# A four-layer graph network on one core: the last LayerNorm, gamma, beta and residual move into the edge pass

## The reference, cut to what matters

```python
h = relu(layernorm(x))
feat = concat([h[src], edge_attr])                 # 100000 x 131
m    = gelu(feat @ W1 + b1) @ W2 + b2              # one message per edge
t    = h + segment_sum(m, dst)                     # 6250 x 128
x    = x + layernorm(t) * gamma + beta             # the output
```

## Time and profile before

| | us |
|---|---|
| median of 3 runs | 6101.89 (6098.71 to 6105.08) |
| the profiled execution | 6096.41 |
| its span, first to last instruction | 6094.7 |
| first step of the edge pass on DVE | 5111.58 |
| last window of the edge pass on DVE | 6053.81 |
| first gather of the edge pass | 5071.93 |
| last gather of the edge pass begins | 6037.01 |

### The profile page before, as it was taken

One profiled execution on the slowest core, in us unless ns is written; L12 is line 12 of the kernel. 1 busy time (PEld: TensorE's weight loads), 2 busy tenths in 40 slices (PEclk: granted clock), 3 DMA queues, 4 the chain that ended last, 5 costly groups with the idle time before them and its releaser, 6 DMA issues. The chain is left out here.

```text
span 6094.7 us, 132845 instructions
## 1 busy us (share of the span) xinstructions
PE 3875.0 (64%) x27584; PEld 3373.1 (55%) x27585; DVE 3724.8 (61%) x9159; ACT 1637.2 (27%) x4058; POOL 4523.9 (74%) x5174
## 2 busy tenths in 40 slices
PE   1555555555555476776789989946666664666765
PEld 1444545445554365655578878845555553545543
DVE  6333333566666677777887787775555555555555
ACT  1000000122121333333455565531111113222222
POOL 6777777677777677777778888857777775777775
PEclk9667666666666688888899999977777776888887
DMA  4222222222222355555577777732222221222222
GB/s 123 69 69 72 71 69 72 62 71 69 72 69 71 104 178 170 174 174 169 174 241 251 248 225 248 251 105 69 71 72 69 71 70 54 72 72 74 70 72 96
DMA packets 457819, 701.26 MB, mean 115 GB/s; under 512 B 94129, under 2 KB 214334, under 8 KB 456690
## 3 DMA queue, kind: packets, MB, share of 16 engines
q0 software_dynamic: 126336, 260.69, 16.6%
q10 hardware_dynamic: 210816, 255.92, 12.9%
q1 hardware_dynamic: 120434, 182.52, 9.2%
HBM read 506.59 MB, written 189.53 MB: 114 GB/s over the span
## 5 line engine op out<-in xcount | busy, mean ns | idle before, releaser
L865 POOL DMA_INDIRECT u_parts<-table,src x3096 | 2921.3, 944 | 1057.8 <-issue 942.9
L941 PE MATMUL ps_sum<-u_parts,onehot 128*128 x2928 | 651.8, 393 | 687.7 <-SPq L720 575.3
L1480 DVE SCALAR_TENSOR_TENSOR onehot<-dst,minus_row,beside 128x512 f32<-128x512 f32 x1100 | 817.4, 744 | 362.2 <-issue 290.0
L941 PEld LDWEIGHTS ps_sum<-u_parts,onehot 128*128 128x128 f32 x2928 | 574.5, 292 | 763.5 <-issue 762.7
L865 POOL DMA_INDIRECT ring<-table,src x774 | 737.6, 953 | 265.4 <-issue 232.0
L941 PEld LDWEIGHTS ps_sum<-msg,onehot 128*128 128x128 f32 x4896 | 689.6, 212 | 302.3 <-issue 152.8
L941 PE MATMUL ps_u<-u_parts,onehot 128*128 x2928 | 537.6, 345 | 464.3 <-SPq L720 414.7
L941 PE MATMUL ps_sum<-msg,onehot 128*128 128x128 f32 x4896 | 748.3, 301 | 124.6 <-DVE msg L528 93.6
L941 PEld LDWEIGHTS ps_u<-u_parts,onehot 128*128 128x128 f32 x2928 | 477.7, 248 | 511.4 <-issue 510.6
L1779 DVE TENSOR_TENSOR zu<-ps_u,ring 128x512 f32<-128x512 f32 x732 | 502.6, 687 | 339.5 <-SPq L720 161.2
L1019 PE MATMUL ps_u<-WE_attr,attr_t 128*128 128x512 f32 x488 | 317.6, 739 | 324.5 <-ACT attr_t L1337 324.5
(11 more groups left out here) (207 smaller groups left out, 6446.1 us busy)
## 6 DMA issues: line engine op xcount, KB each, us to landing
ring<-z_rows SPq DMA_DIRECT2D x392, 256.0 KB, 3.5
ring<-table SPq DMA_DIRECT2D x4096, 0.5 KB
hot_rows<-hots ACTq DMA_DIRECT2D x244, 256.0 KB
hots<-hot_rows ACTq DMA_DIRECT2D x244, 256.0 KB, 3.4
z_rows<-ring SPq DMA_DIRECT2D x196, 256.0 KB
u_parts<-table,src POOLq DMA_INDIRECT x3096
table<-hots ACTq DMA_DIRECT2D x122, 256.0 KB
wide<-hot_rows ACTq DMA_DIRECT2D x122, 256.0 KB, 3.3
```

What stands on the lines that cost most here:

```text
L865: nc.gpsimd.indirect_dma_start(out=slot(p, c % slots)[:, t * P:(t + 1) * P], out_offset=None, in_=tables[p], in_offset=bass.IndirectOffset ...
L941: last = nc.tensor.matmul(sums[k % len(sums)][:, 0:P], lhsT=(onehot[:, k % HOTS, :, :] if hots_of is None else hots_of)[:, t, :], rhs=rows ...
L1480: V.scalar_tensor_tensor(out=buffers[k % len(buffers)], in0=per_row(dst[:, ds(chunk * TILES, TILES)], [P, TILES, P]), scalar=minus_row0[:, ...
```

## The change

The tail behind the edge pass goes away; its work runs per window inside the pass, with the same helpers as in the mean pass.

```diff
@@ act: edge pass
                 if on(k, 7) and have(7):
                     copy_turned(s, 3, 7)
                 if on(k, 11) and have(11):
-                    store_window(s, y_rows[:, blocks_at(act, s, 11, chunk), :], win_y, win_out,
-                                 s.back(11) + (3 * STEPS + UNROLL))
-            over_steps(act, ENGINE.Activation, body, 11)
-            norm_rows(x, acc, groups=0)
-            for g in SCALAR_NORMS:
-                act.wait_ge(y_in[g // 4], 16)
-                norm_group(x, acc, ACT.Identity, g)
+                    root_window(s, 2, 11)
+                if on(k, 13) and have(13):
+                    act.wait_ge(win_rows_ready, s.back(13) + 2 * STEPS)
+                    norm_window(s, 2, 13, win_y, blocks_at(act, s, 13, chunk), ACT.Identity)
+                if on(k, 15) and have(15):
+                    store_window(s, out.rearrange("p (b f) -> p b f", f=P)[:, blocks_at(act, s, 15, chunk), :],
+                                 win_rows, win_rows_ready, s.back(15) + (2 * STEPS + UNROLL))
+            over_steps(act, ENGINE.Activation, body, 15)
@@ dve: edge pass
                 if on(k, 10) and have(10):
                     win = blocks_at(dve, s, 10, chunk)
-                    dve.wait_ge(rows_stored, s.back(10).in_rounds(16, 16 * WINDOWS * 3))
+                    dve.wait_ge(win_normed, s.back(10) + 2 * STEPS)
                     V.tensor_tensor(win_y, x[:, win, :], product_of(s, 3, 10), ALU.add)\
                      .then_inc(win_out, UNROLL)
...
-            over_steps(dve, ENGINE.DVE, edge_body, 10)
+                    window_moments(s, 3, 2, 10, win_y)
+                if on(k, 12) and have(12):
+                    window_scales(s, 2, 12, blocks_at(dve, s, 12, chunk))
+                if on(k, 14) and have(14):
+                    at = s.back(14)
+                    win = blocks_at(dve, s, 14, chunk)
+                    dve.wait_ge(win_normed, at + (2 * STEPS + UNROLL))
+                    V.tensor_tensor(scaled_p, win_h, ga_p.unsqueeze(1).to_broadcast([P, GROUP, P]), ALU.mult)\
+                     .then_inc(win_biased, UNROLL)
+                    dve.wait_ge(win_biased, at + (3 * STEPS + UNROLL))
+                    dve.wait_ge(rows_stored, at.in_rounds(16, 16 * WINDOWS * 3))
+                    V.tensor_tensor(win_rows, scaled_p, h[:, win, :], ALU.add).then_inc(win_rows_ready, UNROLL)
+            over_steps(dve, ENGINE.DVE, edge_body, 14)
```

More of the change, by code:

```diff
@@ L235, in build @@
         caps_p = ps_c[:, 0:GROUP * CAPS]
-        ga_p = beside[:, 0:P]
+        ga_p = beside[:, P:2 * P]
+        scaled_p = ps_c[:, :].rearrange("p (t f) -> p t f", f=P)
         plain_sums = (ps_sum[0], ps_sum[1], ps_u[0], ps_u[1])
@@ L251, in build @@
         hot_rows = nc.dram_tensor("hot_rows", [STEPS, P, 2 * TILES * P], bf16, kind="Internal").ap()
-        y_rows = nc.dram_tensor("y_rows", [P, NB * P], fp32, kind="Internal").ap()\
-            .rearrange("p (b f) -> p b f", f=P)
         z_rows = nc.dram_tensor("z_rows", [CHUNKS, P, TILES * P], fp32, kind="Internal").ap()
@@ L332, in build @@
         h_in = [sem(f"h_in{q}") for q in range(PIECES)]
[L333 to L336, removed]
         root_in = sem("root_in")
@@ L585, in build @@
         CUTS = [(g, min(g + 4, GROUPS)) for g in range(0, GROUPS, 4)]
-        assert len(CUTS) == len(y_in)
-        VECTOR_NORMS = (3, 7, 11, 12)
-        SCALAR_NORMS = [g for g in range(GROUPS) if g not in VECTOR_NORMS]
         NORMED = [0, GROUPS, GROUPS + NORM_GROUPS, 2 * GROUPS + NORM_GROUPS]
@@ L766, in _ @@
             sp.wait_ge(rows_stored, 16 * WINDOWS * 4)
[L767 to L774, removed]
         @block.gpsimd
@@ L870, in _ @@
                     messages(2, messages(1))
[L872 to L875, removed]
         @block.tensor
@@ L1870, in _ @@
             V.tensor_copy(bo_p, BO[:, :])
+            V.tensor_copy(ga_p, GA[:, :])
             link(V.tensor_copy(bt_p, BT[:, :]))
@@ L1911, in edge_body @@
-                    last.then_inc(win_counted, UNROLL)
-                    dve.wait_ge(win_counted, s.back(10) + (STEPS * 2 + UNROLL))
-            over_steps(dve, ENGINE.DVE, edge_body, 10)
-            dve.wait_ge(step_added, STEPS * (EDGE + 1))
[L1915 to L1930, removed]
+                    window_moments(s, 3, 2, 10, win_y)
```

## The result

| | before | after |
|---|---|---|
| median | 6102.89 us (6098.71 to 6105.08, 6 runs) | 6204.43 us (6201.39 to 6211.07, 6 runs) |
| span of the profiled execution | 6094.7 us | 6201.2 us |
| mean granted clock | 0.790 | 0.787 |

The changed kernel takes 1.0168 times as long (95% interval 1.0157 to 1.0179), 101.5 us more. The forecast was 6272 us, +170. The direction, the bound and the range held; the size of the step per round did not.

A forecast was written before the change was run, and what follows sets the result against it. POOL's gathers at 15.8 us a round bound the kernel, with the steps' ring of waits at 15.34 close behind; 3.6 us a round added 192.2, the end took 22.2, the gamma copy added 0.3: 6272 us, range 6200 to 6420.

The forecast's parts named there:

- The bound and the ring: Edge pass: waits passing between DVE, ACT and PE set each round's 15.34 us; work on them lengthens it one for one.
- POOL's slack: Edge pass: the steps' rounds take 15.34 us against 15.8 for POOL's gathers, so half a microsecond a round is free.
- Term 1: DVE behind `bn_stats`: six small operations from statistics to variance delay the next one-hot and `zu`, 1.0 us a round.
- Term 2: DVE behind the variance: two 128x512 operations for gamma and residual, 1.7 us a round, bounds 1.3 and 2.1.
- Term 3: DVE at age 12: two small scale operations fall where it waits 2.57 us for PE, costing nothing.
- Term 4: ACT between Gelu and `attr_t`: four norm activations of 1.65 us, nearly covered, 0.2 us a round, bounds 0 and 0.6.
- Term 5: ACT behind the copy: square root and two table loads, mostly covered by other waits, 0.2 us a round, bounds 0 and 1.6.
- Term 6: ACT's loop head: loading 20 table values instead of 16 and new windows' addresses, 0.5 us a round, bounds 0.1 and 0.9.
- Sum: Edge pass: all additions per round together, 3.6 us, lengthening a round from 15.34 to 18.94 us.
- Rival D: Edge pass: fewer of the additions count, 2.3 us a round, giving 6197 us; chance 0.03.
- rival B: PE in the edge pass: longer idling delays TensorE's return to 2.4 GHz, 1.9 us more a round, 6382 us; chance 0.06.
- The end: From the fifty-ninth window's statistics to the span's end: 30.4 us instead of 52.6, as the tail and POOL's last additions go.

The follow-up runs named there:

- e2: Changed kernel with one more 128x512 DVE operation between the gamma product and the residual, where the next one-hot and `zu` are waited for: 6233.5 us, 1.0208 times before.
- e3: Changed kernel with one more 128x512 DVE operation in the step before `zu`, where DVE waits for PE anyway: 6209.49 us, 1.0167 times before.
- e7: Kernel before with only the six small variance operations added behind `bn_stats` in every window, results unused: 6180.66 us, 1.0135 times before.
- e1: Changed kernel with Copy in place of the window's square root, so 122 table loads go: 6205.99 us, 1.016 times before.
- e8: Kernel before with the 13 last additions on DVE instead of POOL: 6091.3 us, 0.9989 times before.
- e4: Changed kernel with gamma and residual moved to age 17, a step with idle time, and the store to age 19: 6167.12 us, 1.0097 times before.

## Why the prediction was right, and where it was off

- *The bound and the ring.* Right. POOL's slack of half a microsecond was all there was; e2 and e3 show that place counts. The rounds did not lie 18.5 to 19.5 us apart but 17.1 to 18.9. POOL waited 87 us for slots and not 190, and its last gather begins at 6112.6, not near 6230. That has two causes. The mis-sized step is 67 us of it. The rest is POOL's lead, which the prediction left as it was: before, the last gather begins 5 us ahead of the fifty-ninth window's statistics (6037.0 and 6042.11), now 57 us ahead (6112.6 and 6169.46), since a bound of slots lets POOL keep its ring full.
- *Term 1, six small operations, 1.0.* Right: 1.10, and 1.20 where they stand alone (e7).
- *Term 2, gamma and residual, 1.7.* Too high: 1.36 (2.46 - 1.10), close to the lower bound of 1.3. The first of the pair follows the small ones without a gap, and only the second waits, for 0.24. Two gains had no term at all, 0.16 ahead of `win_y` and 0.13 up to the end of `bn_stats`. Together with them this term carries 0.6 of the error.
- *Term 3, scales.* Right, nothing; they run at 5320.50 behind the square root, ahead of a `zu` that still waits 2.00 us for PE.
- *Term 4, norm, 0.2.* Nothing. It ran behind the second Gelu and ahead of an `attr_t` that PE did not yet need.
- *Term 5, root and table loads, 0.2.* Nothing (0.04, e1). The Trainium skill, "ScalarE: Activation LUTs", section "What ACT_TABLE_LOAD costs", adds a drain of 1380 ns to each load. The rows differ: the root starts 0.01 us behind the end of its load (5318.76 + 1.28 = 5320.04), and the load starts 0.02 behind the end of the copy. By the batching rule of the Trainium skill, same page, section "Table sets: the hidden batching unit", this change was wrong; e1 shows that the change was slower for another reason.
- *Term 6, loop head, 0.5.* Right that it is on the ring, too high in size: 0.27 (the 0.31 between copy and `attr_t` less the 0.04 of term 5), where the load of the values itself grew by 0.29 and 0.36 was computed. The "2.66 us now" from which the prediction foretold 3.2 was an unusually long round; the mean is 2.47, and it became 2.78.
- *Sum.* 3.6 forecast, 2.45 measured (17.79 - 15.34): (3.6 - 2.45) x 58 = 67 us of the 69 by which 170.3 misses 101.5. What failed is the size of the small terms: 2, 4 and 5 came in at or near their lower bounds, 6 at half its value, and the two gains of 0.29 had no term. Rival D (2.3 us, 6197) was nearer than the forecast.
- *The clock, rival B.* In its form (third `ps_u` at 2.07) it did not come: the third takes 1.02. The mean PE part did not change (10.67 and 10.67). That this term was nil was luck, not insight: e4 and e7, with still parts of 6.04 and 5.88 between those of before and after, have PE parts of 11.04 and 11.16. What the rounds are worth is not a smooth function of the work added, and the prediction had no step for that.
- *The end.* -22.2 forecast, -20.9 measured. That POOL's DRAIN closed the span was read rightly: without it there (e8) the kernel before is 0.1% faster. It does not lie wholly behind POOL's last addition, though; 8.4 of its 9.7 us do.

## What to carry to other kernels

Find the ring of waits that makes the round and lay out one round as PE-busy time and the rest; price an added operation by the gap it opens in that ring, not by its engine's busy share. Give nothing for an activation table load that stands in a wait already there, but do price what the loop head itself loads: a body that reached four steps further back cost 0.3 us a round, each time. Take the length of a gap from the mean of many rounds, not from the one on the screen. Where PE idles at the head of each round, the clock makes neighbouring rounds of the same work differ by a microsecond, so a small addition can cost more than its length (1.69 us for 1.20 in e7) and a removal return less (0.74 for 1.11 in e4). Here POOL's DRAIN ended 8.4 us behind POOL's last operation whatever that was, so last work on POOL brings these 8.4 us to the end.

## What was not expected of the hardware

- Six operations of 1.2 us per round cost 84 us over the pass, as they also ended the quicker half of the rounds (e7). Both 128x512 operations, with a gap of 1.47 us, gave back only 37 when taken off the ring (e4), partly because the loop head grew by 0.32 a round, partly because PE's part did by 0.37.
- The kernel before took 6103 us in one job and 7570 us on another chip, where plain MOVEs of SP's sequencer took up to 1.4 us instead of 0.03 to 0.07.
- POOL's DRAIN at the program's end ends 8.4 to 8.5 us behind POOL's last operation, be it an addition (before) or a gather (after, e8). Recorded lengths of 9.7, 10.8 and 23.4 us differ only in how early it starts.
